# The stretch between the two halves of a vision tower on one Trainium2 core, laid anew

## What is computed

```
h = patches(x) @ W + b                               # (64, 64, 256)
h = h + sparse_attention(layernorm(h))               # 16 heads, the 25 best-routed keys of each image
h = h + experts(layernorm(h))                        # shared FFN, and 2 of 8 experts for each token
h = h + polymax_attention(layernorm(h))              # causal, polymax in place of softmax, then a projection
h = h + ternary_ffn(layernorm(h))                    # weights in {-1, 0, 1}; 256 -> 1024 -> 256, gelu between
```

## Time and profile before

| what | before |
|---|---|
| time, median of 3 runs (lowest, highest) | 810.17 us (809.11, 811.44) |
| the profiled execution, its time | 813.9 us |
| its span, first to last instruction | 811.8 us |
| mean granted clock of PE | 0.928 |
| busy: PE, DVE, ACT, POOL | 85%, 76%, 52%, 11% |
| chain that ended last: PE, DVE, ACT, issue | 50%, 19%, 16%, 11% |

### The profile page before, as it was taken

How to read it: one execution, slowest core, us unless ns; L and a number is a source line. 1 busy time by engine, 2 the same in 40 slices (tenths; PEclk the granted TensorE clock), 3 DMA queues, 4 the chain that set the end, 5 groups by cost and what they waited for, 6 DMA issues and landing times.

```text
span 811.8 us, 26981 instructions
## 1 busy us (share of the span) xinstructions
PE 691.7 (85%) x11581; PEld 492.2 (61%) x11581; DVE 616.6 (76%) x1393; ACT 425.7 (52%) x653; POOL 89.3 (11%) x76
## 2 busy tenths in 40 slices
PE   5878999999999999965783789899999998888766
PEld 4565676767685858654372557565767665565634
DVE  6676878888888888688477777878979896656643
ACT  4535455554546373543324484956667682745413
POOL 0101212020202020100000101001010100000000
PEclk9889999999999999986875999999999999999959
DMA  9025202020201000200000000000000000000000
GB/s 313 34 77 185 80 0 78 0 78 0 78 0 58 19 0 2 105 2 1 0 2 2 1 3 27 3 28 2 26 0 0 26 3 27 2 27 2 29 1 27
DMA packets 8547, 27.40 MB, mean 34 GB/s; under 512 B 3617, under 2 KB 4385, under 8 KB 6945
## 3 DMA queue, kind: packets, MB, share of 16 engines
q1 hardware_dynamic: 8480, 26.42, 9.1%
HBM read 22.22 MB, written 4.19 MB: 33 GB/s over the span
## 4 chain that ended last, share of the span: by engine, by line
PE 50%; DVE 19%; ACT 16%; issue 11%; SPq 2%; DMA 1%; POOL 1%; DVEq 0%; ACTq 0%; POOLq 0%
PE PS L378 7%; PE PS L327 6%; PE PS L389 5%; PE PS L488 4%; PE PS L717 3%; PE PS L368 3%; PE PS L763 3%; PE PS L477 3%; PE PS L432 3%; DVE mx L1351 3%; DVE Pm L1357 3%; ACT w_s L1056 3%; PE PS L751 2%; PE PS L443 2%; PE PS L707 2%
## 5 line engine op out<-in xcount | busy, mean ns | idle before, releaser
L920 ACT ACTIVATE PT<-PS 128x512 f32<-128x512 f32 x64 | 36.7, 596 | 70.2 <-PE PS L477 70.2
L730 PE MATMUL PS<-xT,wqkv_h 128*128 128x512 f16 x256 | 64.1, 398 | 9.1 <-DVE xT L1729 4.6
L368 PE MATMUL PS<-ident_s,xn 128*128 128x128 f32 x256 | 43.7, 303 | 25.7 <-DVE xn L1272 12.6
L327 PE MATMUL PS<-tokW_h,w_s 128*128 128x256 f16 x504 | 58.5, 273 | 0.0
L913 ACT ACTIVATE Pm<-Pm 128x1024 f32<-128x1024 f32 x32 | 33.1, 1054 | 46.7 <-DVE Pm L1357 46.7
L730 PEld LDWEIGHTS PS<-xT,wqkv_h 128*128 128x128 f16 x256 | 23.4, 101 | 47.7 <-ACT w_s L1056 16.2
L368 PEld LDWEIGHTS PS<-ident_s,xn 128*128 128x128 f32 x256 | 31.1, 150 | 34.8 <-ACT vbuf L1023 11.1
L327 PEld LDWEIGHTS PS<-tokW_h,w_s 128*128 128x128 f16 x504 | 48.6, 98 | 5.8
L443 PE MATMUL PS<-kM,qT 32*64 32x128 f32 x2048 | 51.6, 292 | 0.0
L1260 DVE BATCH_NORM_STATS2 st<-H 128x6 f32 (+1 forms) x128 | 46.3, 413 | 2.5
L477 PE MATMUL PS<-ident_s,Pm 128*128 128x128 f32 x256 | 41.1, 297 | 7.3 <-DVE Pm L1357 7.0
(11 more groups left out here) (250 smaller groups left out, 1587.7 us busy)
## 6 DMA issues: line engine op xcount, KB each, us to landing
work<-in_x SPq DMA_DIRECT2D x7, 1536.0 KB, 6.4
out<-H SPq DMA_DIRECT2D x8, 512.0 KB, 2.6
w_s<-in_w SPq DMA_DIRECT2D x3, 1024.0 KB, 6.9
work<-in_x SPq DMA_DIRECT2D x3, 512.0 KB, 5.5
wup_s<-in_wup SPq DMA_DIRECT2D x1, 1024.0 KB, 6.2
wdn_s<-in_wdn SPq DMA_DIRECT2D x1, 1024.0 KB, 6.9
w_s<-in_tokW SPq DMA_DIRECT2D x3, 256.0 KB, 4.1
wup_s<-in_wqkv SPq DMA_DIRECT2D x1, 768.0 KB, 7.7
```

Of the source, the lines that this page charges most:

```text
L327: m = pe.matmul(dst, halves_[xi][:, k, rows], w[:, wi, k, cols], start=(n == 0), stop=(n == 3 * chunks - 1))
L368: m = pe.transpose(PS[:, bank, t * P:(t + 1) * P], xn[:, t, c * P:(c + 1) * P], ident_s[:, :])
L730: m = pe.matmul(PS[:, UP_BANKS[f % 3], :], wup_h[:, c, f * P:(f + 1) * P], part[:, c, :], start=(k == 0), stop=(k == 2 * C - 1))
```

## The change

All of it is a new order, with the same arithmetic except in the expert choice, which is written in fewer and wider operations, and in pieces.

- Into the last round of the loop go `stats3(0)`, `minus_mean3(0)` and the constants of `setup_B` on DVE, and the two sums of |w| on ACT (`sum_abs`). In every round POOL's `p_bias` moves in front of `p_rstd` and `p_mask`.
- After the loop DVE does `soft(7, 2)` and `soft(7, 3)` first, then the four `attend`. ACT normalizes slot 0 (`a_norm3(0)`, in place of DVE's `norm3`), and PE turns slot 0's rows between the two pairs of softmax tiles, into banks 4 and 5.
- POOL takes the two comparisons of the ternary weights (2048 columns each) and the clearing of `vbuf`; DVE's two ternary passes go to two later places.
- The products of slot 0's second half come before and around slot 7's turn (`turn2`), and the first two score tiles before the shared FFN's last product. ACT takes the first squares and linear parts.
- The expert choice is split: `expert_scores` and `group_choice` stay ahead of `slot_B(0)` (the 18 operations of the group duels become 9), `best` goes into `slot_B(0)`, `second_best` to its end; the weights and row starts go to POOL (`expert_weights`, `row_starts`) and `row_codes`, with 3 operations for 16, into `slot_B(1)`. The two tables go into `slot_B(0)`, one on either side of the scores.

```diff
             with pool.Fori(0, LAST) as i:
                 p_rstd1(i + 1)
+                p_bias(i + 1)
                 p_rstd(ve2_ok, i + 1, ve2, rstd2, rstd2_ok)
                 p_mask(i + 1)
-                p_bias(i + 1)
             p_rstd(ve3_ok, 1, ve, rstd, rstd3_ok)
-            p_rstd(ve2_ok, SLOTS, ve2, rstd2, rstd2_ok)
+            pool.wait_ge(th_set, 2)
+            for n, w in enumerate((wup_f, wdn_f)):
+                pool.tensor_scalar(spare[:, n, :], w, nthr[:, n:n + 1], None, ALU.is_lt).then_inc(th_neg, 1)
+            for p in range(2):
+                ts = slice(2 * p, 2 * p + 2)
+                pool.wait_ge(ve2_ok, LAST + p + 1)
+                pool.tensor_tensor(rstd2[:, ts], ve2[:, ts], mhalf[:, ts], ALU.pow).then_inc(rstd2_ok, 1)
+            pool.wait_ge(pv_mm, 2 * TILES * SLOTS)
+            pool.memset(vbuf[:, :], 0.0).then_inc(V2_zero, 1)
             p_rstd(ve3_ok, 2, ve, rstd, rstd3_ok)
+
+            def expert_weights():
+                pool.wait_ge(cnt_ok, 1)
+                for k, (oh, ck) in enumerate((("oh1", "c1"), ("oh2", "c2"))):
+                    cols = slice(k * NT, (k + 1) * NT)
+                    pool.tensor_scalar(ei[:, cols], rsm[ck][:, :], -1.0, float(NX), ALU.mult, ALU.add)\
+                        .then_inc(choice_step, 1)
+                    pool.tensor_tensor(r3["a"], r3[oh], r3["pr"], ALU.mult).then_inc(choice_step, 1)
...
             def slot_B(g, prev, nxt, routed=None, ahead=True):
+                if routed == "first":
+                    expert_weights()
+                    row_starts()
                 if prev:
                     p_rg(g - 1)
```

On PE and DVE, after the loop:

```diff
             scores(LAST, 1)
             pe.wait_ge(abs_ok, 2)
+            pe.matmul(PS[:, 7, 0:2], ones[:, :], sabs[:, :], start=True, stop=True).then_inc(setup_mm, 1)
             pe.wait_ge(h3_ok, 2 * LAST + 1)
...
             attend_first(LAST, False)
-            pe.wait_ge(pt_out, 2 * (TILES * LAST + 2))
-            attend_second(LAST, lambda c: transpose_chunk(0, c, xn1, FIRST_BANKS[c], xn3_ok, x3T_mm))
-            pe.wait_ge(setup_b, 6)
+            for c in range(C):
+                transpose_chunk(0, c, xn1, FIRST_BANKS[c], xn3_ok, x3T_mm)
+            attend_second(LAST, lambda c: None)
             pe.wait_ge(low_w, PARTS + len(splits) - 1)
+            B1_qk(0, False)
             pe.wait_ge(y_out, TILES * SLOTS)
-            B1_qk(0, False)
+            B1_v(0, (0, 1))
             turn2(LAST, True)
+            B1_v(0, (2, 3))
             A4(LAST, True)
-            pe.wait_ge(h3_ok, 2 * SLOTS + 1)
-            B1_v(0, range(TILES))
-            B2_scores(0, 0)
-            B2_scores(0, 1)
-            routed_tables()
             slot_B(0, False, True)
...
-            setup_B()
+            thresholds()
+            soft(LAST, 2)
+            soft(LAST, 3)
             attend(LAST, 0)
-            soft(LAST, 2)
             attend(LAST, 1)
-            soft(LAST, 3)
-            stats3(0)
-            norm3(0)
+            last_stats2(0)
+            v_x3T(0)
             attend(LAST, 2)
             attend(LAST, 3)
...
-            expert_choice(first_polys)
-            dve.wait_ge(tab_ok, 1)
-            dve.tensor_tensor(tabA[:, 1, :], PS[0:64, 4, 0:P], tabA[:, 0, :], ALU.subtract).then_inc(tab_lo_ok, 1)
-            row_codes()
+            ternary(1, wdn_f, wdn_t)
+            empty_sums()
+            group_choice()
             slot_B(0, False, True)
```

More of the change, by code:

```diff
@@ L550, in A4 @@
                 proj_T(4, s3_h, P, (x4_hi, x4_lo), b_mm)
-                if not last:
+                if last:
+                    pe.wait_ge(x8_ok, 2)
+                    pe.wait_ge(setup_b, 6)
+                    B2_scores(0, 0)
+                    B2_scores(0, 1)
+                else:
                     scores(g + 1, 0)
@@ new lines, in row_starts @@
+            def row_starts():
+                for k in range(2):
+                    pool.memset(off[:, k, 0:4], 0.0).then_inc(choice_step, 1)
+                pool.wait_ge(choice_step, after("choice", 2))
+                pool.wait_ge(cnt_ok, 2)
+                for k, d in enumerate((1, 2, 4)):
+                    src, dst = off[:, k % 2, :], off[:, 1 - k % 2, :]
+                    pool.tensor_tensor(dst[:, 4:4 + NX], src[:, 4:4 + NX], src[:, 4 - d:4 + NX - d], ALU.add)\
+                        .then_inc(choice_step, 1)
+                    pool.wait_ge(choice_step, after("choice"))
@@ L1485, in slot_A @@
                     low_patches(i + 2, (1,))
+                else:
+                    setup_B()
                 v_A4(i)
+                if not more:
+                    minus_mean3(0)
                 soft(i + 1, 0)
@@ new lines, in group_choice, with best @@
+                dve.tensor_tensor(m4, s4, gd[:, :, :].unsqueeze(3).broadcast_to([P, NT, 4, 2]), ALU.add)\
+                    .then_inc(routed_step, 1)
+                dve.wait_ge(routed_step, after("routed"))
+            def best(src, oh, mxk, ck):
+                dve.tensor_reduce(rsm[mxk][:, :], r3[src], AX.X, ALU.max).then_inc(routed_step, 1)
+                dve.wait_ge(routed_step, after("routed"))
+                dve.tensor_tensor(r3["a"], r3[src], each(rsm[mxk]), ALU.is_equal).then_inc(routed_step, 1)
+                dve.wait_ge(routed_step, after("routed"))
+                dve.tensor_tensor(r3["a"], r3["a"], experts(rev8_s), ALU.mult).then_inc(routed_step, 1)
+                dve.wait_ge(routed_step, after("routed"))
+                dve.tensor_reduce(rsm[ck][:, :], r3["a"], AX.X, ALU.max).then_inc(routed_step, 1)
+                dve.wait_ge(routed_step, after("routed"))
+                dve.tensor_tensor(r3[oh], r3["a"], each(rsm[ck]), ALU.is_equal).then_inc(routed_step, 1)
+                dve.wait_ge(routed_step, after("routed"))
@@ L1569, in expert_choice, with second_best @@
+            def second_best():
+                dve.scalar_tensor_tensor(out=rs["b"][:, :], in0=rs["oh1"][:, :], scalar=-BIG, in1=rs["m"][:, :],
+                                         op0=ALU.mult, op1=ALU.add).then_inc(routed_step, 1)
+                dve.wait_ge(routed_step, after("routed"))
+                best("b", "oh2", "m2", "c2")
                 dve.tensor_tensor(rs["a"][:, :], rs["oh1"][:, :], rs["oh2"][:, :], ALU.add).then_inc(routed_step, 1)
@@ L1778, in slot_B @@
                     dve.wait_ge(weighted_ok, g - 1)
+                elif routed == "first":
+                    row_codes()
+                    dve.wait_ge(code_ok, 1)
                 if routed in ("first", "batch"):
@@ L1788, in slot_B @@
                     sums_in(g)
+                if not prev:
+                    best("m", "oh1", "m1", "c1")
                 norm4(g, 0)
@@ L1808, in slot_B @@
                 v_x4T(g)
+                if not prev:
+                    second_best()
                 if nxt:
```

323 lines of the change are left out of this document (164 added, 159 removed).

## The result

The changed kernel takes 785.41 us (median of 4 runs, 780.38 to 787.78), the kernel before 810.81 us in the same session (4 runs, 809.11 to 813.22): a ratio of 0.9667, with a 95% interval from 0.9625 to 0.971. 781.0 was forecast, with a range from 766 to 789. The profiled execution took 786.8 us; its span is 784.6 us against 811.8, at a mean granted clock of 0.948 against 0.928.

The account below looks back on a forecast made before the run. PE was taken to bound the loops, DVE the stretch between them. The terms -45.3 + 1.2 + 1.6 + 0.2 + 10.0 + 0.7 + 1.5 + 0.9 = -29.2, off the 810.2 median, gave 781.0 us; range 766 to 789.

Parts of the forecast that it names:

- The stretch: Between the loops, slot 7's scores to slot 0's polymax of tile 2: gives back 45.3 us, before port and clock terms.
- From here DVE has no gap: After the split of hs, DVE works without waiting: 19.2 us from 385.8 to 405.0, plus 0.7 for the projection.
- The comparisons: POOL's two ternary-weight comparisons near 357: 3 to 4.7 us each, delaying the first `attend` additions 0 to 2, taken as +0.7.
- 0.7 and 0.9: Terms in the stretch: +0.7 for additions waiting on POOL's comparisons, +0.9 for one clock fall after PE idles.
- The port in the rounds: Seven loop rounds: DVE's addition of tile 2 waits for POOL's earlier bias; 0 or +10.0 us, upper end taken.
- Nothing absorbs it: In the loop: nothing later in a round is free of the delayed chain, so all seven rounds lose: +10.0.
- The rival of 768.8: DVE does not wait for POOL, so the 10.0, 0.7 and 1.5 go: 768.8 us, chance 0.26.
- What came back later: Work moved into slots 0 and 1: `best` +1.2, `second_best` 0, `row_codes` +1.6, count's copy +0.2.
- the 1.5 for `expert_weights`: Ten small POOL operations among DVE's polymax and gelu parts contend for the port: 0 to 3.5, taken as +1.5.
- Half clock through the whole first part: Rival: PE stays at half clock from 356.1 to 381.0, doubling 12.5 us of products: 793 us, chance 0.08.
- Slow comparisons: Rival: POOL's comparisons beyond 7.5 us each delay slot 7's rows; 22 each uses up the gain, 30 gives 826; chance 0.03.
- no shortening: Rival: expert choice still stands ahead of what PE needs, so the stretch is not shortened: 808 us, chance 0.03.

Follow-up runs that it names:

- the second trace: Profiled execution (781.1 us) of the changed kernel run again unaltered; that rerun's time was 787.04 us, 0.968 of the kernel before.
- the pieces: Changed kernel with each of POOL's two comparisons of 2048 columns cut into four of 512: 780.81 us, 0.9607 of the kernel before.
- the first trace: Profiled execution (786.8 us) of the changed kernel as first measured, nothing altered; median 785.41 us, 0.9667 of the kernel before.

## Why the prediction was right, and where it was not

- *The stretch.* Right in kind: the named waits went, and what DVE did behind the split of hs came nearly as counted (16.3 us from 396.64 to the end of the group choice at 412.94, where 17.1 were reckoned). The step that failed is "From here DVE has no gap". DVE waits 4.41 us for PE, since PE's table products, which moved into `slot_B(0)`, were in no term of the sum. At the clock of the second trace they leave the stretch at 41.8 us gained (from `sabs` to the polymax 53.3, less 3.1 than the 56.4 of the first), and DVE's wait is 1.14 there; at half clock, 38.7. The polymax of tile 2, foretold near 416, starts at 420.76. No run undoes a part of the stretch itself: how its gain divides among the removed waits, the shorter expert choice and the work moved out is read from rows, not shown by an experiment.
- *The comparisons.* The term was mis-sized. They took 5.45 us each where 3 to 4.7 was the estimate, and the second caught the first addition. The wait that this made cost PE 1.7 us and the half clock behind it 1.7 more (3.4, by the pieces), where 0.7 and 0.9 stood; that half clock came with most such waits and not with all. These two steps, 3.1 and 1.8, are 4.9 of the 5.0 us by which the stretch missed -43.7. The `rstd2` behind them were not late, as the prediction reckoned below 7.5 us.
- *The port in the rounds.* The disputed term, 0 or 10.0, decided for the upper end. The addition ran 1.64 longer, of which PE's wait shows 1.25 (forecast 1.4), and the bias period is 44.06 to 44.18 where no product was slow (forecast 44.3). The loop lost 8.5 and not 10.0. "Nothing absorbs it" was wrong for one round: round 1 took 45.89 from one first projection to the next (70.52 to 116.41), where it was 46.73 before (68.95 to 115.68), so it absorbed its share and the fall of the clock in it; the other fall costs 1.2 in a later round. What bounds round 1 instead stays open. The rival of 768.8 falls with this. The Trainium skill ("SBUF — State Buffer", section "Who interferes with whom") has whichever instruction issues first hold the pair to its end; by that rule the term was 10.0, and the rounds' rows agree but for 0.1 us. The comparison's do not quite: the addition behind it took 3.73, so, at 0.42 for itself, it got in near 374.1, 1.9 us before the comparison's record ends.
- *What came back later.* `best` +0.9 (1.2), and `slot_B(1)` +2.7 (3.3), with `row_codes` at 1.5 by its rows (1.6). Of the 1.5 for `expert_weights` DVE's rows beside it show some 0.8: three passes of 1024 columns, at 445.89, 450.67 and 452.46, took 1.34, 1.75 and 1.37 us for 1.22. The wait of 1.12 ahead of slot 0's norm is gone; `second_best` cost nothing that the table shows.
- *Other rivals.* Half clock through the whole first part: not so; the clock was 0.57 from 378 to 382, and 1.00 from 382 to 399. Slow comparisons and no shortening: not so. The price put on the slow ones was misread: 22 us for 2048 columns is ten times a whole bias, and 4.7 times its 2.3 ns a column.
- *The time.* -27.2 for -29.2 in the profiled spans looks closer than it is: the stretch missed by 5.0, the loop by 1.5 the other way, and every later stage by a little. Between the medians it is -25.4, since the profiled execution of before (813.9) lay 3.1 above its median of four runs and that of after 1.4.

## What to carry to other kernels

A wide GpSimd instruction is not free because its engine is idle: look at what VectorE starts while it runs, and follow the held instruction to the engine that awaits it. Cutting it into pieces made the cost vanish here in both places, with no reordering, though POOL itself took longer. And when work is moved into a stretch that shrinks, cost every engine's moved work, not that of the bounding engine alone: where the clock was low, the next bound was PE's small products, which no row of the old stretch showed as a wait. Before an edit is credited with a few microseconds, look whether the same instructions ran at the same clock in both traces.

## What the hardware showed

- DVE's normalization (one SBUF tensor, two pointers) waits for POOL as its additions of two tensors do: two took 2.29 us for 0.73 beside a clearing that only writes, four took 3.41 for 1.38 beside the bias. Its passes over one tensor in SBUF and one in PSUM did not wait: those of 512 columns took 0.69 us beside the bias (at 302.94 and 303.80, in the kernel before) and 0.68 and 0.69 without it (at 353.57 and 354.28, in the changed one).
- POOL's comparison of one tensor with a pointer took 2.66 ns a column (5.45 us for 2048), its addition of two tensors 2.30 (2.35 us for 1024).
- The granted clock of one stretch differs between executions of the same kernel: 0.50 (the lower level) or 0.90 over the same table products, 6.84 or 3.95 us. In the first trace it fell during the first table, at 0.80 from 399.4 to 404.0, while PE was busy without a pause. Two traces of one kernel differ by 3 us for that reason alone, and two traces of two kernels can.
